# VectorE's order in the linear-attention loop: when the output is added to X, and when its statistics and moments are taken

## The chip, the cores and the metric

The kernel runs on one core of one Trainium2 chip, as one launch. The metric is the device time of that launch in microseconds. Before the change three runs took 624.18, 625.54 and 626.89 us; their median is 625.54 us.

## What is computed

A decoder block over x of shape 128 x 64 x 128 (batch, sequence, features), three sublayers, each added to x:

```
x = x + attention(layernorm(x))            # linear attention, 16 heads of 8, causal
x = x + correlation(layernorm(x), context) # lags picked from correlations, then mixed
x = x + moe(layernorm(x))                  # 8 experts, 2 for each row
```

The change lies in the first sublayer. For each head, with q, k passed through relu and exp and v plain:

```
S_t = sum over s <= t of k_s v_s^T ;  z_t = sum over s <= t of k_s
out_t = (q_t S_t) / (q_t z_t + eps) ;  x = x + out @ wo + bo
```

The correlation sublayer needs the mean and variance of the new x of each row, for its own layernorm.

## The kernel before

The 8192 rows are 64 tiles of 128 rows (two sequences in each), in 16 groups of 4 tiles. X, the running activations, stays in SBUF for all rows. Attention is a software pipeline over the groups, written by hand: each engine has a function `slot(n, i)`, called for n = -2 to 17 (slots 4 to 13 in a loop of two slots a turn, the others unrolled). In slot n an engine works on up to five groups at once: `a0` = n+2 (statistics and normalisation of the attention's input), `a1` = n+1 (transposes, projections, features, outer products), `b` = n (running sums over time and their product with q), `c` = n-1 (division, output product, add to X, statistics of the new X), `d` = n-2 (normalisation of the new X, keys, Gram matrices for the correlation sublayer). Each engine's instructions run in the order in which its `slot` writes them; engines meet through semaphores only.

What each engine does in a slot, as far as the prediction's steps touch it:

- TensorE (L1392): transposes of `xh` for a1 (L1353), running sums of tile 1 of b, projection 0, key sums, projection 1, transposes of `on` for c, running sums 2, keys of d, output product of c (which lets go `c_y`), projection 2, transposes of `xh` for d (the buffer `xh2`), running sums 3, projection 3, running sums 0 of the next group, Gram products of d (which wait for `c_x1`). All matrix products go through one helper and have line L1349.
- ScalarE (L681): evacuates the projections (L656 to L661), copies `xT` and `oT`, and normalises: `nb_a`, `xh` for a0, `nb_c`, `xh` for d (both through L675 and L678), which wait for GpSimd's roots `rs_a` and `rs_c`.
- GpSimd (L553): features `qk` (L540), outer products (L549), and between them the variances `ve_a`, `ve_c` (L525), each waiting for VectorE's moments, and the roots `rs_a`, `rs_c` (L531).
- VectorE (L965): for each tile of b a product `R` of the running sums with q (L899, `times_q`) and its sum over the head's elements `num` (L909, `sum_heads`). `R` is a single buffer: a product waits for the sum before it, and a sum for its own product. In between: reciprocals (L948) and quotients `on` (L954) of c, key dots `zq`, `den` of b (L915, L922), statistics and moments of a0 (L876, L884), the add of the output product to X (L962, `add_attention`, waits for `c_y`), and statistics and moments of the new X (L876, L884 with `st_c`, `mv_c`).

The running sums alternate between two PSUM buffers, so TensorE can be at most two tiles ahead of VectorE's products. Behind the 16 groups the correlation sublayer begins with a reduction over stored Gram matrices (`mean_early`), which needs the last group.

Of the kernel before, what the change touches and what calls it, by code (L numbers as in the profile page):

```python
# [55 lines left out]
def need(eng, sem, count):  # L56

    if not (isinstance(count, int) and count <= 0):
        eng.wait_ge(sem, count)
# [7 lines left out]
def build(nc, x, ctx_t, ctx_r, wqkv_p, b_all, wo, wq2, wk2, wv2t, wo2, bq2, bk2, bv2, scale, w_router, w_experts,  # L67
          tri, stri, ident, iota, dest, walk, place, late_in, out):
    with ExitStack() as ctx:
# [256 lines left out]
        def stage(n, i, shift):  # L326

            if i is None and not 0 <= n + shift < NG:
                return None
            return grp(n + shift, i)  # L330
# [503 lines left out]
        def _(dve):  # L834
            def fold_projection():

                dve.wait_ge(const_in, 64)
                dve.wait_ge(w_mean, 1)
                nc.vector.tensor_tensor(b_wide, b_wide, bank[1][:, 0:3 * E], ALU.subtract).then_inc(w_ch, 1)
                dve.wait_ge(w_ch, 1)  # L840
                nc.vector.scalar_tensor_tensor(wqkv[:], b_wide, 1.0 / E, wqkv[:], ALU.mult, ALU.add).then_inc(w_ch, 1)

            def fold_queries():

                nc.vector.tensor_reduce(q_shift[:, 0:1], wq2_s[:], AX.X, ALU.add).then_inc(kk_ch, 1)
                dve.wait_ge(kk_ch, 1)
                nc.vector.tensor_tensor(q_shift[:, 1:2], bq2_s[:], q_shift[:, 0:1], ALU.subtract).then_inc(kk_ch, 1)
                dve.wait_ge(kk_ch, 2)
                nc.vector.tensor_scalar(q_shift[:, 2:3], q_shift[:, 1:2], 1.0 / E, None, ALU.mult).then_inc(kk_ch, 1)
                dve.wait_ge(kk_ch, 3)  # L850
                nc.vector.tensor_scalar(wq2_s[:], wq2_s[:], q_shift[:, 2:3], None, ALU.add).then_inc(kk_ch, 1)

            def split_biases():

                n = 0

                def step(ins):
                    nonlocal n
                    n += 1
                    ins.then_inc(bias_ch, 1)  # L860
                    dve.wait_ge(bias_ch, n)
                step(nc.vector.tensor_copy(bias_p[0][:], bias_f))
                step(nc.vector.tensor_tensor(bias_r, bias_f, bias_p[0][:], ALU.subtract))
                step(nc.vector.tensor_copy(bias_p[1][:], bias_r))
                step(nc.vector.tensor_tensor(bias_a, bias_r, bias_p[1][:], ALU.subtract))
                step(nc.vector.tensor_copy(bias_p[2][:], bias_a))
                step(nc.vector.tensor_scalar(bias_b, bias_p[0][:], id_s[0:3, 0:1], None, ALU.mult))
                step(nc.vector.scalar_tensor_tensor(bias_r, bias_p[1][:], id_s[0:3, 1:2], bias_b, ALU.mult, ALU.add))
                dve.wait_ge(padded, 2)
                step(nc.vector.scalar_tensor_tensor(bias3[0:3, :], bias_p[2][:], id_s[0:3, 2:3], bias_r, ALU.mult, ALU.add))  # L870

            def stats(g, p, st, st_sem, mv, mv_sem, seen, per_group):
                need(dve, mv_sem, GT * g)
                settle(dve)
                for k in range(GT):
                    nc.vector.bn_stats(st[:, k, :], X[:, bass.ds(GT * g + k, 1), :].rearrange("p a b -> p (a b)")  # L876
                                       ).then_inc(st_sem, 1)

            def moments(g, p, st, st_sem, mv, mv_sem, seen, per_group):
                dve.wait_ge(st_sem, GT * g + GT)  # L880
                need(dve, seen, per_group * (g - 1))
                settle(dve)
                for k in range(GT):
                    nc.vector.bn_aggr(mv[p][:, k, :], st[:, k, :]).then_inc(mv_sem, 1)  # L884
# [9 lines left out]
            def times_q(g, p, r, k):  # L894
                t = GT * g + k
                need(dve, b_red, t)
                dve.wait_ge(b_run, t + 1)
                qq = qk[p][:, k, 0:E].rearrange("p (h d) -> p h d", h=H)
                nc.vector.tensor_tensor(  # L899
                    R[:, 0:D * E].rearrange("p (h e d) -> p h e d", h=H, e=D),  # L900
                    run[k % 2][:].rearrange("p (h e d) -> p h e d", h=H, e=D),
                    qq.unsqueeze(2).broadcast_to([P, H, D, D]), ALU.mult).then_inc(b_mul, 1)

            def sum_heads(g, p, r, k):
                t = GT * g + k
                dve.wait_ge(b_mul, t + 1)
                if k == 0:
                    need(dve, c_on, g - 1)
                nc.vector.tensor_reduce(num[p][:, k, :], R[:, 0:D * E].rearrange("p (x d) -> p x d", d=D), AX.X, ALU.add  # L909
                                        ).then_inc(b_red, 1)  # L910

            def key_dots(g, p, r):

                dve.wait_ge(b_keys, g + 1)
                nc.vector.tensor_tensor(  # L915
                    zq[:].rearrange("p (k c x) -> p c k x", k=GT, c=2), bank[4][:].rearrange("p (c k x) -> p c k x", c=2, k=GT),
                    qk[p][:, :, 0:E].rearrange("p k (c x) -> p c k x", c=2), ALU.mult).then_inc(b_dots, 1)

            def sum_dots(g, p, r):
                dve.wait_ge(b_dots, 2 * g + 1)  # L920
                need(dve, c_rden, g)
                nc.vector.tensor_reduce(den[:], zq[:].rearrange("p (x d) -> p x d", d=D), AX.X, ALU.add).then_inc(b_dots, 1)  # L922
# [21 lines left out]
            def inverses(g, p, r):  # L944
                dve.wait_ge(c_den, g + 1)
                need(dve, d_gd, g - 1)
                need(dve, c_x1, g)
                nc.vector.reciprocal(rden, den[:]).then_inc(c_rden, 1)  # L948

            def quotients(g, p, r):  # L950
                dve.wait_ge(c_rden, g + 1)
                need(dve, c_tr, g)
                dve.wait_ge(b_red, GT * g + GT)
                nc.vector.tensor_tensor(  # L954
                    on[:].rearrange("p t (h d) -> p (t h) d", h=H), num[p][:].rearrange("p t (h d) -> p (t h) d", h=H),
                    rden.unsqueeze(2).broadcast_to([P, GT * H, D]), ALU.mult).then_inc(c_on, 1)
# [8 lines left out]
            def slot(n, i):  # L965
                a0, a1, b, c = (stage(n, i, s) for s in (2, 1, 0, -1))
                if b:
                    times_q(*b, 0)
                    sum_heads(*b, 0)
                if c:  # L970
                    if i is None and c[0] == 0:
                        dve.wait_ge(kk_w, 1)
                    inverses(*c)
                if b:
                    times_q(*b, 1)
                if c:
                    quotients(*c)
                if b:
                    key_dots(*b)
                if a0:  # L980
                    g, p, r = a0
                    dve.wait_ge(x_in[p], 16 * r + 16)
                    stats(g, p, st_a, a_st, mv_a, a_mv, a_nb, GT)
                if b:
                    sum_heads(*b, 1)
                    sum_dots(*b)
                if a0:
                    moments(a0[0], a0[1], st_a, a_st, mv_a, a_mv, a_nb, GT)
                if i is None and n == FIRST:
                    fold_projection()  # L990
                    split_biases()
                if i is None and n == -1:
                    dve.wait_ge(w_in, N_W)
                    nc.vector.tensor_copy(bv2_wide[:], bv2_s[:, 0:1].broadcast_to([P, P])).then_inc(fold_wide, 1)
                    fold_queries()
                if i is None and n == NG:
                    split_fold()
                if b:
                    times_q(*b, 2)
                if c:  # L1000
                    add_attention(*c)
                if b:
                    sum_heads(*b, 2)
                if c:
                    dve.wait_ge(c_x1, c[0] + 1)
                    stats(c[0], c[1], st_c, c_st, mv_c, c_mv, c_nb, GT)
                if b:
                    times_q(*b, 3)
                if c:
                    moments(c[0], c[1], st_c, c_st, mv_c, c_mv, c_nb, GT)  # L1010
                if b:
                    sum_heads(*b, 3)

            slots(dve, slot)

            dve.wait_ge(w_in, N_W)
# [745 lines left out]
```

## Time and profile before

| | |
|---|---|
| median of the runs | 625.54 us |
| the profiled execution's own time | 626.32 us |
| its span, first to last instruction | 624.1 us |
| granted TensorE clock, mean | 0.979 |
| busy: TensorE, VectorE, ScalarE, GpSimd | 556.2, 504.1, 417.6, 407.6 us |

An engine's busy share says how much it does, not whether others wait for it; that is read from the idle times with their releasers, and from the chain of work that ended last. The attention stage fills the span's first 270 us.

### The profile page before, as it was taken

The page shows a single profiled execution, that of the slowest core. Times are in us where ns is not written, and L with a number is a line of the kernel's source. Part 1 is how long each engine was busy: PE and PEld are TensorE (multiplying, and loading weights), DVE is VectorE, ACT ScalarE, POOL GpSimd, SP SyncE. Part 2 cuts the span into 40 slices and gives each one's busy share as a digit, 9 for nine tenths or more (in the row PEclk, how much of TensorE's full clock was granted, in tenths as well). Part 3 has the DMA queues.
Part 4 walks back from the last instruction along what each step waited for, and adds up shares of the span by engine and source line. Part 5 has one row for each costly group of instructions (what it writes and reads, how often), then busy time and mean ns, then how long its engine had stood idle before and what let it go on. Part 6 is the DMA issues. An engine that isn't in the chain of part 4 may idle for free.

```text
span 624.1 us, 16569 instructions
## 1 busy us (share of the span) xinstructions
PE 556.2 (89%) x4286; PEld 407.8 (65%) x4287; DVE 504.1 (81%) x1506; ACT 417.6 (67%) x1188; POOL 407.6 (65%) x459
## 2 busy tenths in 40 slices
PE   4888999999999998878899786899999999999993
PEld 1333444444444444445888544799999999999993
DVE  4489999999999999874578988466887878877883
ACT  3556878888888775532888502445887888878882
POOL 2778888888888888112877501764566766757762
PEclk9979999999999999899999969999999999999998
DMA  5510111111161112362568480221111111111110
GB/s 153 187 50 2 35 35 36 35 34 34 34 101 34 34 37 65 67 137 57 159 196 206 78 137 5 59 51 38 35 50 51 47 44 47 52 40 51 52 45 22
DMA packets 49973, 40.99 MB, mean 66 GB/s; under 512 B 21971, under 2 KB 40278, under 8 KB 49926
## 3 DMA queue, kind: packets, MB, share of 16 engines
q1 hardware_dynamic: 44150, 29.68, 19.5%
q0 software_dynamic: 4960, 10.49, 6.4%
q8 instruction: 21, 0.34, 0.2%
q10 hardware_dynamic: 816, 0.26, 0.2%
q14 instruction: 26, 0.21, 0.1%
HBM read 27.54 MB, written 12.88 MB: 65 GB/s over the span
## 4 chain that ended last, share of the span: by engine, by line
PE 55%; ACT 16%; DVE 10%; issue 10%; POOL 4%; DMA 3%; ACTq 0%; SPq 0%; DVEq 0%; POOLq 0%
PE bank L1349 30%; PE run L1349 19%; ACT xh L678 4%; PE bank L1353 4%; ACT xs L780 2%; ACT ex L656 2%; DMA shared<-xs_d,row_u 2%; ACT nb_a L675 2%; PE run L1616 1%; ACT ex L661 1%; DVE mean_early L1057 1%; ACT xT L649 1%; PE run L1540 1%; DMA ct<-in_ctx_r 1%; ACT rl L657 1%
## 5 line engine op out<-in xcount | busy, mean ns | idle before, releaser
L616 POOL DMA_INDIRECT shared<-xs_d,row_u x91 | 87.8, 965 | 62.6 <-DVE row_u L1247 31.6
L549 POOL TENSOR_TENSOR shared<-v,qk 128x1024 f32<-128x1024 f32 x64 | 125.0, 1953 | 2.8
L623 POOL DMA_INDIRECT out_x<-shared x64 | 63.5, 992 | 48.2 <-DVE shared L1319 22.1
L899 DVE TENSOR_TENSOR R<-run,qk 128x1024 f32<-128x1024 f32 x64 | 77.5, 1210 | 12.5 <-PE run L1349 11.0
L1349 PE MATMUL bank<-wqkv,xT 128*64 128x128 f32 (+1 forms) x384 | 70.5, 353 | 15.5 <-ACT v L659 10.8
L1349 PEld LDWEIGHTS bank<-wqkv,xT 128*64 128x64 f32 (+1 forms) x384 | 33.4, 159 | 72.1 <-issue 37.4
L909 DVE TENSOR_REDUCE num<-R 128x128 f32<-128x1024 f32 x64 | 77.2, 1206 | 1.1
L1349 PE MATMUL run<-shared,tris_s 64*64 64x512 f32 x512 | 73.3, 644 | 0.0
L809 ACT ACTIVATE shared<-run,scale_s 128x128 f32<-128x128 f32 (+1 forms) x78 | 30.0, 385 | 41.5 <-PE run L1616 41.5
L540 POOL TENSOR_TENSOR qk<-ex,rl 128x256 f32<-128x256 f32 x64 | 46.5, 727 | 11.0 <-DVE mv_a L884 7.5
L656 ACT ACTIVATE ex<-bank 128x256 f32<-128x256 f32 x64 | 24.1, 376 | 28.9 <-PE bank L1349 28.9
L1349 PE MATMUL run<-w_s,hid 128*128 (+1 forms) x312 | 41.4, 275 | 0.0
L1349 PE MATMUL bank<-w_s,hid 128*128 (+1 forms) x308 | 41.1, 276 | 0.0
L813 ACT ACTIVATE ct<-w_s 128x512 f32 x64 | 39.8, 621 | 0.3 <-issue 0.3
L1340 DVE TENSOR_TENSOR hid<-run,shared 128x256 f32<-128x256 f32 x78 | 33.0, 423 | 8.3 <-ACT shared L819 7.9
L1349 PEld LDWEIGHTS run<-w_s,hid 128*128 128x128 f32 x312 | 38.0, 192 | 0.1
L1349 PEld LDWEIGHTS bank<-w_s,hid 128*128 128x128 f32 x308 | 37.6, 192 | 0.4 <-DVE hid L1340 0.2
L819 ACT ACTIVATE shared<-run 128x256 f32<-128x256 f32 x78 | 29.8, 382 | 10.9 <-PE run L1349 7.7
L819 ACT ACTIVATE shared<-bank 128x256 f32<-128x256 f32 x77 | 29.5, 383 | 10.9 <-PE bank L1349 8.6
L1340 DVE TENSOR_TENSOR hid<-bank,shared 128x256 f32<-128x256 f32 x77 | 32.5, 422 | 3.2 <-ACT shared L819 3.0
L1349 PE MATMUL run<-shared,ct 128*128 128x128 f32 x256 | 33.9, 275 | 0.0
L1349 PE MATMUL bank<-shared,ct 128*128 128x128 f32 x256 | 33.9, 275 | 0.0
(277 smaller groups left out, 1425.1 us busy)
## 6 DMA issues: line engine op xcount, KB each, us to landing
xs_d<-xs SPq DMA_DIRECT2D x16, 270.0 KB, 5.2
X<-in_x SPq DMA_DIRECT2D x16, 256.0 KB, 2.7
ct<-in_ctx_t SPq DMA_DIRECT2D x16, 256.0 KB, 3.0
ct<-in_ctx_r SPq DMA_DIRECT2D x16, 256.0 KB, 3.7
gram_d<-gd SPq DMA_DIRECT2D x14, 256.0 KB, 2.4
w_s<-in_w_experts SPq DMA_DIRECT2D x8, 384.0 KB, 3.9
circ<-prob_d SPq DMA_DIRECT2D x30, 64.0 KB, 2.8
shared<-xs_d,row_u POOLq DMA_INDIRECT x91, 2.6
```

The source lines that it names most:

```text
L540: nc.gpsimd.tensor_tensor(qk[p][:, k, :], ex[k % 2][:], rl[k % 2][:], ALU.add).then_inc(a_f, 1)
L549: nc.gpsimd.tensor_tensor(outer[k].rearrange("p (h e d) -> p h e d", h=H, e=D), vv.unsqueeze(3).broadcast_to([P, H, D, D]), kk.unsqueeze(2 ...
L616: nc.gpsimd.indirect_dma_start(xg[q], None, xs_d[:, :], bass.IndirectOffsetOnAxis(ap=rows, axis=0)).then_inc(xg_in[q], 16)
L623: nc.gpsimd.indirect_dma_start(out[:, :], bass.IndirectOffsetOnAxis(ap=xg[(NXI + j) % NX][:, DEST:DEST + 1].bitcast(U32), axis=0), yg[q], ...
L656: nc.scalar.activation(ex[k % 2][:], bank[1][:, HALF:HALF + 2 * E], ACT.Relu, scale=-1.0).then_inc(a_pev, 1)
L809: nc.scalar.activation(xgT[p][:, cols], bank[0][:, cols], ACT.Copy, scale=scale_s[:, 0:1]).then_inc(x_xT, 1)
L813: nc.scalar.activation(w_tile[n % 2][0], w_s[:, dyn(held[0] * W_E, 2 * HID)], ACT.Copy).then_inc(x_wa, 1)
L819: nc.scalar.activation(silu[p][h], bank[1 + 2 * p + h][:, HID:2 * HID], ACT.Silu).then_inc(x_silu, 2 // len(items_of(i, up[0])))
L899: nc.vector.tensor_tensor(R[:, 0:D * E].rearrange("p (h e d) -> p h e d", h=H, e=D), run[k % 2][:].rearrange("p (h e d) -> p h e d", h=H, ...
L909: nc.vector.tensor_reduce(num[p][:, k, :], R[:, 0:D * E].rearrange("p (x d) -> p x d", d=D), AX.X, ALU.add).then_inc(b_red, 1)
L1340: nc.vector.tensor_tensor(hid[p][h][:], bank[1 + 2 * p + h][:, 0:HID], silu[p][h], ALU.mult).then_inc(x_h, 2 // len(items_of(i, j)))
L1349: return nc.tensor.matmul(o, l, r, start=start, stop=stop, skip_group_check=True)
```

## The change

Only VectorE's `slot` changes. Nothing is added or removed; four things change places. The order of the second half of a slot was

times_q 2, add_attention, sum_heads 2, stats (new X), times_q 3, moments (new X), sum_heads 3

and becomes

times_q 2, sum_heads 2, add_attention, times_q 3, stats (new X), moments (new X), sum_heads 3.

```
                 if b:
                     times_q(*b, 2)
+                    sum_heads(*b, 2)
                 if c:
                     add_attention(*c)
                 if b:
-                    sum_heads(*b, 2)
+                    times_q(*b, 3)
                 if c:
                     dve.wait_ge(c_x1, c[0] + 1)
                     stats(c[0], c[1], st_c, c_st, mv_c, c_mv, c_nb, GT)
-                if b:
-                    times_q(*b, 3)
-                if c:
                     moments(c[0], c[1], st_c, c_st, mv_c, c_mv, c_nb, GT)
                 if b:
                     sum_heads(*b, 3)
```

Where b or c is missing (slot 0 and before, slots 16 and 17) the order stays as it was.

## Rows read from the trace of the kernel before

**Rows 1.** Busy time of each engine, 100 to 240 us, with clock and DMA share.
```profile
100.00:240.00 140.00, 130.24 (x932) 63.66 (x930) 133.80 (x268) 111.14 (x376) 121.81 (x114) 1.00 0.19 45
```

**Rows 2.** Shares of the chain of waits by line, 100 to 240 us.
```profile
by line: PE bank L1349 34.7%; ACT xh L678 12.2%; issue 11.6%; PE bank L1353 10.4%; ACT ex L656 4.5%; ACT ex L661 4.5%; PE run L1349 4.4%; ACT nb_a L675 3.8%; ACT xT L649 3.5%; ACT rl L657 2.5%; ACT gd L726 2.3%; ACT nb_c L675 1.6%; ACT den 
```

**Rows 3.** Time line of VectorE, slots 9 and 10: start, duration, line, operation.
```profile
164.55 1.19 DVE L899 TENSOR_TENSOR R<-run,qk 128x1024 f32<-128x1024 f32 x1
166.06 0.69 DVE L962 TENSOR_TENSOR X<-X,bank 128x512 f32 x1 [0.32 <-PE bank L1349]
166.67 1.21 DVE L909 TENSOR_REDUCE num<-R 128x128 f32<-128x1024 f32 x1
167.80 0.86 DVE L876 BATCH_NORM_STATS2 st_c<-X 128x6 f32 x4
168.57 1.21 DVE L899 TENSOR_TENSOR R<-run,qk 128x1024 f32<-128x1024 f32 x1
...
171.31 1.23 DVE L899 TENSOR_TENSOR R<-run,qk 128x1024 f32<-128x1024 f32 x1
172.65 1.22 DVE L909 TENSOR_REDUCE num<-R 128x128 f32<-128x1024 f32 x1
...
175.37 0.68 DVE L954 TENSOR_TENSOR on<-num,bank 128x512 f32<-128x512 f32 x1
...
179.06 0.37 DVE L884 BATCH_NORM_AGGREGATE mv_a<-st_a 128x2 f32<-128x6 f32 x4
...
183.38 1.21 DVE L899 TENSOR_TENSOR R<-run,qk 128x1024 f32<-128x1024 f32 x1
```

**Rows 4.** Idle time before the X add (L962): total us, times.
```profile
  PE bank L1349: 5.6, 13
```

**Rows 5.** Time line of slot 15: TensorE's transposes, VectorE's X add.
```profile
249.89 1.12 PE L1353 MATMUL bank<-id_s,on 128*128 128x128 f32 x4 [1.56 <-DVE on L954]
...
255.21 0.69 DVE L962 TENSOR_TENSOR X<-X,bank 128x512 f32<-128x512 f32 x1 [0.92 <-PE bank L1349]
```

**Rows 6.** Time line of TensorE, slots 9 and 10.
```profile
164.85 1.05 PE L1349 MATMUL bank<-wo_s,oT 128*128 128x128 f32 x8
...
167.27 1.09 PE L1349 MATMUL run<-shared,tris_s 64*64 64x512 f32 x8
...
170.77 0.69 PE L1349 MATMUL bank<-x2T,k2T 128*64 128x64 f32 x16
...
171.84 0.65 PE L1353 MATMUL bank<-id_s,xh 128*128 128x128 f32 x4 [0.39 <-ACT xh L678]
...
176.87 0.66 PE L1353 MATMUL bank<-id_s,on 128*128 128x128 f32 x4
...
182.16 1.09 PE L1349 MATMUL run<-shared,tris_s 64*64 64x512 f32 x8
```

**Rows 7.** Time line of VectorE, slot 16: statistics directly before moments.
```profile
265.58 0.87 DVE L876 BATCH_NORM_STATS2 st_c<-X 128x6 f32<-128x128 f32 x4 [0.19 <-DVE X L962]
266.64 0.38 DVE L884 BATCH_NORM_AGGREGATE mv_c<-st_c 128x2 f32<-128x6 f32 x4 [0.18 <-DVE st_c L876]
```

**Rows 8.** Time line of GpSimd: slot 0, then slots 9 and 10.
```profile
34.40 1.02 POOL L531 TENSOR_TENSOR rs_a<-ve_a,power 128x4 f32<-128x4 f32 x1
...
167.70 1.02 POOL L531 TENSOR_TENSOR rs_a<-ve_a,power 128x4 f32<-128x4 f32 x1
...
179.63 0.19 POOL L525 TENSOR_SCALAR ve_a<-mv_a 128x4 f32<-128x4 f32 x1 [1.73 <-DVE mv_a L884]
...
182.50 1.02 POOL L531 TENSOR_TENSOR rs_a<-ve_a,power 128x4 f32<-128x4 f32 x1
```

**Rows 9.** Time line of ScalarE: slot 0, then slots 9 and 10.
```profile
35.45 0.85 ACT L675 ACTIVATE nb_a<-mr_a,rs_a 128x1 f32<-128x1 f32 x4 [0.84 <-POOL rs_a L531]
...
169.32 0.85 ACT L675 ACTIVATE nb_a<-mr_a,rs_a 128x1 f32<-128x1 f32 x4
...
184.21 0.85 ACT L675 ACTIVATE nb_a<-mr_a,rs_a 128x1 f32<-128x1 f32 x4
```

More of the change, by code:

```diff
@@ L999, in slot @@
                     times_q(*b, 2)
+                    sum_heads(*b, 2)
                 if c:
@@ L1002, in slot @@
                 if b:
-                    sum_heads(*b, 2)
+                    times_q(*b, 3)
                 if c:
@@ L1006, in slot @@
                     stats(c[0], c[1], st_c, c_st, mv_c, c_mv, c_nb, GT)
-                if b:
-                    times_q(*b, 3)
-                if c:
                     moments(c[0], c[1], st_c, c_st, mv_c, c_mv, c_nb, GT)
```

## The prediction

> **What bounds the kernel now.** I read the busy shares of the attention loop first, then the chain of waits of the same stretch, then the time lines of the engines over two neighbouring slots, one odd (slot 9) and one even (slot 10), and last what the instructions at the changed place wait for. The change touches only slots in which both a group in its running-sum stage and a group in its output stage exist: slots 1 to 15. Between 100 and 240 us VectorE is busy 133.80 us of 140 and TensorE 130.24 [rows 1]; shares alone would name VectorE. The chain says otherwise: it consists of TensorE and ScalarE pieces (projection and its evacuations, `xh`, transposes), and no VectorE line is among its largest [rows 2]. The clock in that stretch is the full one, 1.00 of 2.4 GHz [rows 1]. One slot is the distance between the multiplications `R` of the third tile: 164.55 here, and the odd slot's X add at 166.06 carries the wait that the change wants to be rid of, 0.32 us for TensorE's output product [rows 3]. There are 13 such waits with 5.6 us in all over the stage [rows 4], and slot 15's alone is 0.92 [rows 5].
>
> **The changed order, priced on slot 9.** Before, VectorE starts: product 2 at 164.55, X add 166.06, sum 2 166.67, statistics 167.80, product 3 168.57, next slot's product 0 171.31 [rows 3]. The steps between independent neighbours are 1.13 us behind a product or a sum (166.67 to 167.80), 0.61 behind the X add, 0.77 behind four statistics: each is about 0.09 shorter than the instruction, because the next one starts before it has ended. Nothing is added or removed in count; three things change.
>
> (a) Sum 2 now stands right behind product 2, which it needs. Product 0 and sum 0 stand like that already: 171.31 to 172.65, 1.34 us instead of 1.13 [rows 3], so +0.21. X add then starts at 164.55 + 1.34 + 1.13 = 167.02. The output product's last record ends at 164.85 + 1.05 = 165.90 [rows 6] and before let the X add go at 166.06, 0.16 later; so the 0.32 wait is gone. VectorE would be ready for product 3 at 167.02 + 0.61 = 167.63, 0.94 earlier than before.
>
> (b) Product 3 can't use that. It reads the fourth tile's running sums, which TensorE makes from 167.27 to 168.36 [rows 6]; with the same 0.16 for the release it starts at 168.52, against 168.57 before. VectorE idles 0.89 us there. In slot 10 the sums end at 182.16 + 1.09 = 183.25 [rows 6], release 183.41, against 183.38 before [rows 3]: +0.03. This is the wait that takes the place of the one removed. TensorE's sums are in turn fed by nothing that the change brings forward: ahead of them stand the projection and the transposes of ScalarE's `xh`.
>
> (c) What was done while VectorE waited for those sums is now behind product 3: the statistics, and right behind them the moments, which need them. The trace has this pair adjacent, in slot 16: 265.58 to 266.64, 1.06 us, of which 0.18 is noted as idle for the statistics [rows 7]; between independent neighbours it is 0.77. So behind product 3 everything on VectorE starts 1.06 us later: in slot 9 by 1.06 - 0.05 = 1.01 us, in slot 10 by 1.06 + 0.03 = 1.09 us. Bounds for this lag: 0.77, if the gap of 0.29 is hidden, and 1.3, if the loop's register work adds as much again as the 0.21 of (a).
>
> The Trainium skill (VectorE: DVE Perf Modes, section The DRAIN you can't avoid) says that a semaphore between chained VectorE operations costs nothing extra, and its table advises to minimize the count of operations, not the semaphores. Here the trace does not agree: 1.34 against 1.13 and 1.06 against 0.77 for the dependent pairs. By that rule the lag would be 0.72 and 0.80, and the sum made below would be 1.4 + 0.76 = 2.1 us, a time of 627.7 instead of 629.7.
>
> **Who waits for VectorE once it is late by 1.0 to 1.1 us.** Queued behind product 3 and late by this lag are: moments of X, sum 3, and in the next slot product 0, sum 0, reciprocals, product 1, the quotients `on`, key dots, statistics and moments `mv_a`, up to product 2. There the lag ends, since 0.89 us of new idle time at product 3 absorbs it; it is made anew in each slot. Three consumers matter.
>
> TensorE's transposes of `on`: after slot 9 `on` ends at 175.37 + 0.68 = 176.05 and TensorE takes it at 176.87 [rows 3, 6]. The slack is 0.82 less a release; a lag of 1.01 costs about 0.2.
>
> GpSimd's variance waits for `mv_a` in every slot: 1.73 us of idle time ending at 179.63, 0.20 behind `mv_a`'s end at 179.43 [rows 3, 8]. So the lag passes whole into its outer product, features and `rs_a`. `rs_a` ends at 168.72 in slot 9 and 183.52 in slot 10 [rows 8], and ScalarE starts `nb_a` at 169.32 and 184.21 [rows 9]. A release from GpSimd to ScalarE shows as 0.03 (34.40 + 1.02 = 35.42, start 35.45) [rows 8, 9]. Slack: 0.57 in slot 9, 0.66 in slot 10. Behind `nb_a` the four `xh` follow, and TensorE waits 0.39 for them [rows 6], so whatever `nb_a` loses goes into the chain whole.
>
> TensorE's Gram product needs the X add, which now ends by 167.02 + 0.69 = 167.71, or 168.8 with the lag; it starts at 170.77 [rows 6], so two microseconds of TensorE's other work cover it. The moments `mv_c` end about 1 us later than before; GpSimd comes to them late by the same lag, as it is itself held by `mv_a`, so they cost nothing; if that failed, it would be at most the lag in one of GpSimd's pieces, some tenths a slot.
>
> **The sum.** A loop over two slots closes: product 3 of an even slot is late by 1.09 against TensorE, `nb_a` of the next slot by 1.09 - 0.57 = 0.52, that goes through `xh` into TensorE's queue, and the next even slot's running sums, hence its product 3, are 0.52 later. The path over `on` gives 0.2 a pair and runs beside it, hidden by the larger one; the odd slots' 1.01 - 0.66 = 0.35 is smaller than the shift already there. Slots 2 to 13 are six pairs: 6 x 0.52 = 3.1 us. (The first slots, still filling, may give less: bound 5 pairs, 2.6.) In slot 14 no new group is normalised, and slot 15's transposes of `on` wait for VectorE already, 1.56 us [rows 5]: the lag of slot 14, about 1.05, adds whole. In slot 15 the X add loses its wait of 0.92 [rows 5], the two gaps add 0.21 + 0.29 = 0.50, and product 3 may wait for its sums: between -0.4 and +0.5, taken as 0, because in slots 9 and 10 a freed wait is taken up by those sums. Sum: 3.1 + 1.05 = 4.2 us.
>
> The profiled execution took 626.3 (span 624.1 and 2.2 around it), the median of the runs is 625.5. So 630.5 for the profiled one and **629.7 us** for the median. With a lag of 0.8 the same sum gives 2.1, with 1.3 it gives 6 x 0.73 + 1.3 = 5.7: the forecast's own range is 627.6 to 631.2.
>
> **Rivals.**
> 1. Faster: VectorE sets the period, as its busy share suggests. Place: the X add; price: the 5.6 us of waits go, 619.9 us, if the gaps cost nothing; with 15 x 0.50 us of gaps it is +1.9 and no gain at all. It decides if product 3 is released about 0.9 us before the record of its sums allows and the gaps are small. For it: 133.80 busy of 140. Against: the chain has no VectorE, and product 3 already stands within 0.2 us of the end of its sums in both slots. Half of it would be 622.7.
> 2. No change: the lag is made, but ScalarE or GpSimd make it good before TensorE feels it, so that the loop over two slots doesn't close and only the end of the stage pays, 0 to 1.5 us: 625.5 to 627.0. For it: GpSimd has 1.73 us of idle time a slot. Against: that idle time lies ahead of `ve_a`, not behind it.
> 3. Much slower: TensorE, waiting longer in slot 15, runs more of its work at the lower clock. The transposes there took 1.12 us after an idle time of 1.56, against 0.66 for the same four in slot 10 [rows 5, 6]. Another microsecond of idle time could cost 1 to 2 us on top: 631 to 632.
>
> **Chances.** Forecast 0.55, rival 1 0.12, rival 2 0.23, rival 3 0.10. 0.5% is 3.1 us, what a measurement of this kernel can tell from no change. Of the forecast about three quarters lie above 628.7; with rival 3 that gives slower 0.50. Same is the rest of the forecast and rival 2, 0.38; faster is rival 1, 0.12. The range 624.5 to 632.0 holds the forecast, rival 2 and most of rival 3, and leaves out most of rival 1.
>
> **What would show it.** Right: the X add has no idle time in the loop; product 3 has 0.7 to 0.9 us of it per slot, released by TensorE's running sums; statistics to moments 1.0 to 1.1 us; `nb_a` waits for `rs_a` in odd slots; the slot is 14.8 us before (168.57 to 183.38) and near 15.1 after; GpSimd's idle time ahead of `ve_a` stays or grows. Wrong: if product 3 starts 0.9 us earlier against its running sums, step (b) is false; if statistics to moments is 0.9 or less, step (c) is too dear; if `nb_a` isn't late, the loop over two slots isn't there.

## The result, and the profile after

The changed kernel takes 629.14 us (median of 10 runs, 628.63 to 631.28) against 625.48 us before (10 runs). The ratio is 1.0059 with a 95% interval of 1.0037 to 1.0082: slower by 3.7 us. Forecast were 629.7 us and +4.2. The profiled execution has a span of 627.2 us, 3.1 more than before.

First the same busy row as in [rows 1], of the changed kernel, 100 to 240 us.

```profile
100.00:240.00 140.00, 126.47 (x919) 63.08 (x919) 134.34 (x268) 108.74 (x368) 120.09 (x112) 1.00 0.19 45
```

VectorE is as busy as before (134.34 us), TensorE is less so (126.47 for 130.24) at the same full clock: it waits more. Then the chain of the same stretch, of whose largest pieces in [rows 2] none was VectorE's or GpSimd's.

```profile
by line: issue 32.9%; DVE R L899 8.9%; ACT xh L678 7.7%; PE bank L1347 6.8%; POOL qk L540 5.2%; PE bank L1351 4.0%; DVE num L909 3.7%; POOL rs_a L531 3.5%; PE run L1347 3.4%; DVE st_a L876 3.0%; DVE st_c L876 2.5%; ACT ex L656 2.4%; POOL sh
```

Now VectorE's products, sums and statistics stand in it, and GpSimd's `qk` and `rs_a`. VectorE in the same two slots as in [rows 3]:

```profile
167.26 1.19 DVE L899 TENSOR_TENSOR R<-run,qk 128x1024 f32<-128x1024 f32 x1
...
168.49 1.22 DVE L909 TENSOR_REDUCE num<-R 128x128 f32<-128x1024 f32 x1
...
169.62 0.68 DVE L962 TENSOR_TENSOR X<-X,bank 128x512 f32 x1
...
170.44 1.22 DVE L899 TENSOR_TENSOR R<-run,qk 128x1024 f32<-128x1024 f32 x1
...
171.59 0.86 DVE L876 BATCH_NORM_STATS2 st_c<-X 128x6 f32 x4
...
172.63 0.38 DVE L884 BATCH_NORM_AGGREGATE mv_c<-st_c 128x2 f32<-128x6 f32 x4 [0.18 <-DVE st_c L876]
...
172.93 1.19 DVE L909 TENSOR_REDUCE num<-R 128x128 f32<-128x1024 f32 x1
...
174.24 1.22 DVE L899 TENSOR_TENSOR R<-run,qk 128x1024 f32<-128x1024 f32 x1
...
178.31 0.67 DVE L954 TENSOR_TENSOR on<-num,bank 128x512 f32<-128x512 f32 x1
...
182.27 1.19 DVE L899 TENSOR_TENSOR R<-run,qk 128x1024 f32<-128x1024 f32 x1
...
185.55 1.23 DVE L899 TENSOR_TENSOR R<-run,qk 128x1024 f32<-128x1024 f32 x1 [0.24 <-PE run L1347]
```

The X add has no idle time ahead of it (0.32 before). Statistics to moments are 1.04 us here and 1.10 in slot 10, as [rows 7] had 1.06. Product 3 stands at 170.44, where its running sums end at 169.29 + 1.09 = 170.38. Product 2 of slot 10 is late as well (182.27), and from product 3 to product 3 are 15.11 us, where [rows 3] had 14.81. What the other engines waited for in these slots:

```profile
169.29 1.09 PE L1347 MATMUL run<-shared,tris_s 64*64 64x512 f32 x8
...
171.46 0.85 ACT L675 ACTIVATE nb_a<-mr_a,rs_a 128x1 f32<-128x1 f32 x4 [0.22 <-POOL rs_a L531]
...
173.99 0.65 PE L1351 MATMUL bank<-id_s,xh 128*128 128x128 f32 x4 [0.52 <-ACT xh L678]
...
177.27 1.10 PE L1347 MATMUL bank<-qk,tris_s 128*128 128x256 f32 x4 [0.26 <-POOL qk L540]
...
182.55 0.19 POOL L525 TENSOR_SCALAR ve_a<-mv_a 128x4 f32<-128x4 f32 x1 [1.94 <-DVE mv_a L884]
...
184.39 1.09 PE L1347 MATMUL run<-shared,tris_s 64*64 64x512 f32 x8
```

ScalarE's `nb_a` now waits for `rs_a` in slot 9 (in [rows 9] it didn't), TensorE's transposes of `xh` wait 0.52 behind it (0.39 in [rows 6]), GpSimd waits longer for `mv_a` (1.94 after 1.73 in [rows 8]). One wait is new and I hadn't priced it: TensorE's key sums wait 0.26 for the features `qk` of the fourth tile, where before they waited for nothing in the loop. Another row will matter further on: the transposes of `on` start at 179.12, 0.14 behind the end of `on` (178.31 + 0.67). Where a wait for `on` is noted (moments of the input early, below), they start 0.15 behind it. The slack of this path, 0.82 before, is used up to its end. The pieces of the chain over two slots show the loop as a whole. The columns are start and length.

```profile
156.60 0.87 DVE st_c L876 x4
158.08 1.11 DVE num L909
159.31 1.23 DVE R L899
...
162.17 1.19 DVE R L899
164.69 0.66 DVE st_a L876 x3
...
169.73 0.73 POOL qk L540
170.45 0.98 POOL rs_a L531
172.61 0.83 ACT xh L678 x2
...
176.31 0.73 POOL qk L540
177.27 1.90 PE bank L1347 x10
179.17 0.60 PE bank L1351 x4
182.49 1.27 ACT xh L678 x3
...
184.46 1.06 PE run L1347 x8
...
186.69 0.88 DVE st_c L876 x4
```

From statistics to statistics are 186.69 - 156.60 = 30.09 us, two slots of the changed kernel; before they were 29.69 (X add of slot 4 to that of slot 12, four pairs: 91.80 to 210.56). The loop runs: statistics and sum 3 on VectorE, the next slot's products, the statistics of the new group, GpSimd's outer product and features, `rs_a`, ScalarE's `xh`, TensorE, GpSimd's features again, TensorE's key sums and transposes, `xh` of d, running sums 3, product 3.

The stage divided by VectorE's product 0 of slots 1, 4 and 14 and by the start of `mean_early`, us:

| kernel | slots 1 to 3 | slots 4 to 13 | slot 14 to `mean_early` | sum |
|---|---|---|---|---|
| before | 44.6 | 148.4 | 39.2 | 232.2 |
| changed | 46.3 | 150.4 | 39.8 | 236.5 |

4.3 us come up in this stage. The rest of the kernel is the same code and gave 1.2 of it back in this one execution. At the X add of slot 16 the changed kernel is at 268.89, before at 264.71: 4.2 us.

### The profile page after: what moved, and what is told of

It reads as the page before. It is cut to its first block, busy times and chain, and to the rows that moved or that the text cites. A ratio compares the mean times of both kernels' runs of the same rounds, so it can differ in the third digit from the quotient of the medians.

```text
span 627.2 us, 16569 instructions
## 1 busy us (share of the span) xinstructions
PE 554.3 (88%) x4286; PEld 408.5 (65%) x4287; DVE 507.0 (81%) x1506; ACT 417.7 (67%) x1188; POOL 407.3 (65%) x459
## 4 chain that ended last, share of the span: by engine, by line
PE 50%; DVE 17%; issue 13%; ACT 8%; POOL 6%; DMA 4%; DVEq 1%; POOLq 0%; ACTq 0%; SPq 0%
PE bank L1347 24%; PE run L1347 21%; DVE R L899 3%; ACT xh L678 2%; PE bank L1351 2%; ACT xs L780 2%; POOL qk L540 2%; PE run L1614 2%; DMA w_s<-gram_d 1%; DVE num L909 1%; POOL shared L549 1%; DVE mean_early L1055 1%; POOL rs_a L531 1%; DVE st_c L876 1%; PE run L1538 1%
## 5 line engine op out<-in xcount | busy, mean ns | idle before, releaser
L813 ACT ACTIVATE ct<-w_s 128x512 f32 x64 | 39.8, 621 | 0.3 <-issue 0.3
```

The costliest lines, as they stand in the source:

```text
L813: nc.scalar.activation(w_tile[n % 2][0], w_s[:, dyn(held[0] * W_E, 2 * HID)], ACT.Copy).then_inc(x_wa, 1)
```

## The experiments

All are compared with the kernel before on the same chip. "Two slots" is the mean distance of X adds of slots 4 to 12, from the profile. "Stage" is the sum of the three columns above and "end" the last of them. "Reduction" is where `mean_early` starts in the profiled execution; unlike "stage" it holds what happens before slot 1 as well. "Clock" is the granted TensorE clock between 240 and 262 us, slots 14 and 15 in the main, as a share of 2.4 GHz. Between 100 and 240 us it is 1.00 in all twelve.

| kernel | two slots | stage | end | reduction | clock | ratio, interval |
|---|---|---|---|---|---|---|
| before | 29.69 | 232.2 | 39.2 | 269.74 | 0.92 |  |
| changed | 30.10 | 236.5 | 39.8 | 274.11 | 0.92 | 1.0059, 1.0037 to 1.0082 |
| first half only | 29.61 | 233.8 | 40.2 | 271.40 | 0.92 | 1.0015, 0.9995 to 1.0035 |
| second half only | 30.10 | 235.2 | 40.0 | 272.59 | 0.92 | 1.0054, 1.0035 to 1.0073 |
| changed, moments last | 30.00 | 232.7 | 38.5 | 270.13 | 1.00 | 0.9997, 0.9981 to 1.0013 |
| changed, `mv_a` early | 30.08 | 237.3 | 40.2 | 273.95 | 0.92 | 1.0042, 1.0020 to 1.0065 |
| changed, variance later | 30.09 | 234.3 | 39.5 | 270.73 | 0.92 | 1.0026, 1.0002 to 1.0050 |
| changed, quotients early | 30.30 | 236.7 | 38.9 | 274.27 | 0.92 | 1.0058, 1.0035 to 1.0080 |
| changed, both of these | 29.94 | 231.1 | 37.3 | 267.09 | 1.00 | 0.9956, 0.9938 to 0.9975 |
| moments last, variance of X later | 29.82 | 233.8 | 40.6 | 271.33 | 0.84 | 1.0008, 0.9985 to 1.0032 |
| before, quotients early | 29.71 | 229.4 | 37.3 | 266.98 | 1.00 | 0.9963, 0.9938 to 0.9988 |
| first half, both edits | 29.86 | 230.3 | 36.8 | 266.38 | 1.00 | 0.9965, 0.9939 to 0.9990 |

Two things can be read off the table before any theory. The time follows the start of the reduction to within 1.6 us: with both of these edits it comes 2.65 us earlier and the kernel is 2.8 us faster. And the end of the stage goes with the clock. In the four kernels with 1.00 it takes 36.8 to 38.5 us, in the others 38.9 to 40.6. The rows for this stand behind the experiments.

**First half only.**

```diff
                 times_q 2
-                add_attention
                 sum_heads 2
+                add_attention
                 stats ; times_q 3 ; moments ; sum_heads 3
```

> Only the first half of the change: sum 2 stands before the X add, but statistics stay before product 3 and moments behind it. Theory A (the loop over two slots: what is late behind product 3 reaches GpSimd's rs_a and qk, ScalarE's xh and TensorE): the lag behind product 3 is some 0.1 us, under the slack of 0.5 to 0.67, so two slots of the loop take 29.7 us as before and the time is 625.5 us, ratio 0.998 to 1.002. Theory B (VectorE's own queue sets the new period by its length): the waits of 0.32 go, the gaps at sum 2 and at the statistics add about 0.4, so two slots take 29.7 to 29.8, ratio 1.000 to 1.003. Theory C (the later X add is what harms, by itself): two slots take 30.1 as in the changed kernel, ratio 1.006.

Measured: two slots 29.61, ratio 1.0015, an interval that holds 1. Moving the X add behind the sum does no harm in the loop; theory C falls. In the profile the stage is 1.6 us longer all the same: slots 1 to 3 take 1.0 more, the loop 0.4 less and the end 1.0 more. At the end the X add of slot 15 stands at 256.06, after 255.21 before, and the Gram products of that slot at 257.26 after 256.55. Their matrices go out and come back as the diagonal's load, which now lands last, while the X add of slot 16 is where it was (264.70 for 264.71):

```profile
271.40 7.10 DVE L1057 TENSOR_REDUCE mean_early<-w_s 112x64 f32<-112x4096 f32 x1 [1.59 <-DMA w_s<-gram_d]
```

**Second half only.**

```diff
                 times_q 2 ; add_attention ; sum_heads 2
+                times_q 3
                 stats
-                times_q 3
                 moments ; sum_heads 3
```

> Only the second half of the change: the X add stays before sum 2, statistics and moments both stand behind product 3. Theory A: the lag of about 1 us behind product 3 is the same as in the changed kernel, so two slots take 30.0 to 30.1 us, ratio 1.004 to 1.007. Theory B: VectorE's queue has the wait of the X add back or its own gap at product 3 instead of the one at sum 2, about as long: 30.0 to 30.1 too, ratio 1.004 to 1.007. Theory C: as before, 29.7, ratio 1.000.

Measured: 30.10 and 1.0054. The whole loss of the loop sits in the statistics behind product 3, as A and B said. Their times don't tell A and B apart, but the trace does. Product 3 waits in every slot of the loop, 0.27 to 0.36 us, for TensorE's running sums:

```profile
168.64 1.22 DVE L899 TENSOR_TENSOR R<-run,qk 128x1024 f32<-128x1024 f32 x1 [0.27 <-PE run L1349]
...
183.75 1.23 DVE L899 TENSOR_TENSOR R<-run,qk 128x1024 f32<-128x1024 f32 x1 [0.35 <-PE run L1349]
```

So the length of VectorE's queue is not what sets this period.

**Moments behind sum 3**, on the changed kernel (moments last).

```diff
                 times_q 3
                 stats
-                moments
                 sum_heads 3
+                moments
```

> The changed kernel with sum 3 between statistics and moments, so that the gap of 0.27 us ahead of the moments is filled; the moments of X themselves come 0.9 later, which should be covered. Theory A: the lag falls from about 1.0 to 0.75, two slots take 29.69 + 0.41 - 0.27 = 29.8, ratio 1.001 to 1.004. Theory B: the queue is 0.27 shorter in each slot, more than the whole excess, two slots 29.7, ratio 0.999 to 1.001. If the gap is of no account: 30.1, ratio 1.006.

Measured: the time is that of before (0.9997), and yet two slots take 30.00: neither theory's number. VectorE in an even slot, with what waited for it:

```profile
171.33 0.37 DVE L884 BATCH_NORM_AGGREGATE mv_c<-st_c 128x2 f32<-128x6 f32 x4
...
171.90 0.19 POOL L525 TENSOR_SCALAR ve_c<-mv_c 128x4 f32<-128x4 f32 x1 [0.49 <-DVE mv_c L884]
...
175.09 1.10 PE L1349 MATMUL bank<-qk,tris_s 128*128 128x256 f32 x4 [0.35 <-POOL qk L540]
...
183.36 1.23 DVE L899 TENSOR_TENSOR R<-run,qk 128x1024 f32<-128x1024 f32 x1 [0.70 <-PE run L1349]
```

Product 3 has 0.70 us of idle time, so VectorE's queue has room and its length is not the bound: theory B falls for this kernel. But the moments of X are now so late that GpSimd waits 0.49 for them ahead of an outer product, its features come late, and TensorE's key sums wait 0.35: a third route. I had priced the moments at nothing. The stage is 0.5 us longer than before: the loop lost 1.6, slots 1 to 3 gave back 0.4 and the end 0.7. At the end the granted clock stays at 1.00 in this kernel, for 0.92 before.

**Moments of the input early** (`mv_a` early), on the changed kernel.

```diff
                 sum_heads 1
+                moments (a0)
                 sum_dots
-                moments (a0)
```

> The changed kernel with the moments of the attention's input (mv_a) before the reduction of the key dots instead of behind it: mv_a is ready 0.6 us earlier, VectorE's queue keeps all its instructions. Theory A: mv_a's lag of 0.9 to 1.1 falls to 0.3 to 0.5, below both slacks, so the loop over two slots opens; what is left is the path over on, 0 to 0.25 for two slots: 29.7 to 29.9, and the lag at the end of the stage, 1.0 us. Ratio 1.001 to 1.004. Theory B: VectorE's queue is as long as in the changed kernel: 30.1, ratio 1.006.

Measured: two slots 30.08, no change, where A expected 29.7 to 29.9. `nb_a` no longer waits, but this does:

```profile
169.85 1.23 DVE L899 TENSOR_TENSOR R<-run,qk 128x1024 f32<-128x1024 f32 x1
...
177.72 0.67 DVE L954 TENSOR_TENSOR on<-num,bank 128x512 f32<-128x512 f32 x1
...
178.54 0.63 PE L1352 MATMUL bank<-id_s,on 128*128 128x128 f32 x4 [0.16 <-DVE on L954]
...
184.95 1.23 DVE L899 TENSOR_TENSOR R<-run,qk 128x1024 f32<-128x1024 f32 x1 [0.23 <-PE run L1348]
```

Product 3 to the end of `on` is 178.39 - 169.85 = 8.54 us, from there over the transposes (which wait 0.16 for `on`) to the next product 3 are 6.56: 15.10 for this slot, and 30.08 - 15.10 = 14.98 for the next. Theory B's number fits too, but product 3 has 0.23 us of idle time, so the queue is not full. The loop over `on` is as long as the one over `mv_a`; I had put it at 0.2 for two slots and hidden. Theory A as predicted, one route that holds the period, falls; A2, two routes of nearly the same length, is the next to test.

**Variance later**, on the changed kernel: GpSimd stops standing still for `mv_a`; VectorE's order is untouched.

```diff
                 features 0
-                variance (a0)
                 outer_product 0
+                variance (a0)
                 features 1
```

> The changed kernel; only GpSimd's order differs: outer product 0 before the variance of a0, so that GpSimd no longer stands still for mv_a, and rs_a and qk come up to 1.9 us earlier. VectorE's queue is untouched. Theory A as predicted (mv_a is the one route that closes the loop): two slots 29.7 to 29.8. Theory A2 (two routes of nearly the same length, mv_a and on): with this one cut, on alone holds the period, 30.05 to 30.1 for two slots, ratio 1.004 to 1.006; TensorE's transposes of on wait for VectorE in even slots. Theory B (length of VectorE's queue): 30.1 as well, but without TensorE waiting for on.

Measured: 30.09 for two slots, as A2 said. TensorE's transposes wait 0.18 us for `on` in slot 10, and product 3 has 0.23 of idle time there, so theory B isn't the reason. In the chain between 160 and 200 us, shown below, `on` has 5.1% and neither `qk` nor `rs_a` is among the largest. The ratio of 1.0026 lies below the 1.004 to 1.006 that I expected. Product 0 of slot 1 starts 1.2 us earlier than in the changed kernel (36.46 for 37.63) and slots 1 to 3 take 1.8 less (44.5 for 46.3): the edit also speeds up the filling of the pipeline, which has nothing to do with the loop.

```profile
by line: issue 20.5%; PE bank L1348 14.8%; PE run L1348 13.1%; PE bank L1352 9.6%; DVE R L900 9.3%; DVE st_c L877 6.6%; DVE num L910 5.9%; DVE on L955 5.1%; ACT xh L679 3.6%; DVE mv_c L885 2.8%; DVEq L877 1.7%; ACT nb_c L676 1.4%; ACT ex L6
```

**Quotients early**, on the changed kernel.

```diff
                 inverses
-                times_q 1
                 quotients
+                times_q 1
                 key_dots
```

> The changed kernel with VectorE's quotients before product 1 instead of behind it: on is ready about 1 us earlier, product 1 and all behind it up to mv_a 0 to 0.2 us later. Theory A2: the mv_a route is uncut, two slots 30.1 to 30.3, ratio 1.005 to 1.009. Theory C2 (on is the only route in fact): 29.7 to 29.8, ratio 1.001. Theory B: 30.1 to 30.4 (a gap more in the queue).

Measured: 30.30, ratio 1.0058. With only the `on` route cut nothing is won. The chain between 100 and 240 us has the other route instead, over `qk` and `rs_a`, and no `on` among the largest:

```profile
by line: issue 33.9%; ACT xh L678 7.7%; DVE R L899 7.0%; PE bank L1346 6.7%; POOL qk L540 5.2%; DVE num L909 3.7%; PE bank L1350 3.6%; POOL rs_a L531 3.5%; PE run L1346 3.0%; DVE st_a L876 3.0%; DVE st_c L876 2.5%; ACT ex L656 2.4%; POOL sh
```

**Both edits together**, variance later and quotients early, on the changed kernel.

> Both edits together: quotients before product 1 on VectorE, outer product 0 before the variance of a0 on GpSimd, on the changed kernel. Theory A2: both routes are gone, two slots fall to 29.7 to 29.9, held by TensorE and ScalarE or by VectorE's queue with its gaps (about 14.9 a slot); the end of the stage keeps its part: ratio 1.000 to 1.003. Theory B: 30.1 or more, ratio 1.006 or more.

Measured: two slots 29.94, just above the 29.7 to 29.9 of A2, and ratio 0.9956, faster than before and better than the 1.000 to 1.003 expected. Neither edit alone shortened the two slots, both together do, by 0.16: so there are two routes beside each other, A2. The chain of the loop is now VectorE's queue:

```profile
by line: issue 41.4%; DVE R L900 16.9%; DVE num L910 8.4%; DVE st_c L877 5.6%; DVE st_a L877 5.3%; PE bank L1347 3.5%; DVE bank L949 3.2%; DVE mv_c L885 2.4%; DVEq L877 2.4%; DVE mv_a L885 2.4%; PE run L1347 1.5%; DVE zq L916 1.2%; DVE den 
```

So about 14.97 us a slot is what VectorE needs with the gaps of this order, more than the 14.84 of before: 29.94 is its floor, and the excess over 29.69 that stays is theory B's, in this kernel only. Part of this floor comes from the edit itself. The quotients now stand right behind the reciprocals that they need, 0.70 us instead of the 0.46 to the product that stood there. In the changed kernel VectorE has idle time at product 3, so there the floor is not reached. The time is won outside the loop. Before slot 1 it is 1.6 us (product 0 of slot 1 at 35.95 for 37.58), in slots 1 to 3 it is 0.3 and at the end 1.9 (37.3 for 39.2), less the 1.2 lost in slots 4 to 13.

**Moments last and the variance of X later.**

```diff
                 features 2
-                variance (c)
                 outer_product 2
+                variance (c)
                 features 3
```

> The kernel with moments behind sum 3 (two slots 30.0 us there, GpSimd waiting 0.49 for mv_c), with GpSimd's outer product 2 before the variance of the new X. If the route over mv_c, features of tile 3 and the key sums holds its period, two slots fall to 29.7 to 29.8, 1.0 to 1.4 us for the stage, and the kernel is faster than the one before: 624.8, ratio 0.996 to 0.999. If on or mv_a hold it as well: 30.0, ratio 1.000.

Measured: two slots fall from 30.00 to 29.82, so the route over the moments of X was real. The ratio is 1.0008, where 0.996 to 0.999 was expected: the loop's gain of 0.9 us over ten slots was lost again at the end of the stage, which took 40.6 us for 38.5. From the X add of slot 14 to that of slot 15 alone are 16.84, for 14.79. The whole difference lies behind the transposes of `on`, from which to the X add are 6.62 us for 4.57, and there the granted clock is 0.50, as the rows below show. What holds the loop at 29.82 and not at 29.69 is open.

**Quotients early on the kernel before.**

> The kernel before with one edit: quotients before product 1. The run with both routes cut (ratio 0.9956) had a loop of 29.94 us for two slots, 0.25 above before, and yet was faster, since its slots 14 to 16 took 2.9 us less: TensorE waits for on there. If that is the reason, this kernel keeps the loop of before (29.7; VectorE's 0.32 of idle time a slot covers the new gap of about 0.24 ahead of the quotients) and takes 1.5 to 2.5 us off the end of the stage: ratio 0.995 to 0.998. If the gap is not covered: two slots 29.9 to 30.1, ratio 0.998 to 1.001.

Measured: two slots 29.71, ratio 0.9963. The gap ahead of the quotients is covered in the loop, as expected: the X add has no idle time left in even slots, and 0.32 still in odd ones. From the X add of slot 14 to that of slot 15 are 13.37 us for 15.23. This is the smallest edit that beats both kernels.

**First half of the change with both edits.**

> The kernel with sum 2 before the X add and statistics before product 3 (first half of the change, two slots 29.61 us), with both edits that cut the routes. By the theory of the two routes nothing is late behind product 3, and VectorE's queue of about 14.9 us a slot is the floor: two slots 29.7 to 29.9, the end of the stage as in the kernel with both routes cut: ratio 0.994 to 0.997. If the first half of the change cost something at the end of the stage again (the diagonal's load came 1.6 us late there): 0.997 to 1.000.

Measured: 29.86, ratio 0.9965, as expected; no better than the previous one.

**The clock in slot 15.** TensorE's transposes of `on` and the running sums behind them, in the kernel before, then in the kernel before with quotients early, then with moments last and the variance of X later. In the lines that begin with a stretch of time the third number from the end is the granted clock.

```profile
250.94 1.99 PE L1349 MATMUL run<-shared,tris_s 64*64 64x512 f32 x8
...
250.00:252.00 2.00, 2.00 (x12) 0.91 (x12) 2.00 (x3) 0.96 (x4) 0.04 (x1) 0.50 0.03 8
```
```profile
248.01 0.66 PE L1352 MATMUL bank<-id_s,on 128*128 128x128 f32 x4 [0.58 <-DVE on L954]
...
248.60 1.09 PE L1348 MATMUL run<-shared,tris_s 64*64 64x512 f32 x8
...
248.00:250.00 2.00, 1.84 (x13) 0.82 (x14) 2.00 (x3) 1.29 (x6) 1.15 (x1) 1.00 0.16 61
```
```profile
250.23 1.12 PE L1354 MATMUL bank<-id_s,on 128*128 128x128 f32 x4 [2.23 <-DVE on L955]
...
250.00:256.00 6.00, 5.77 (x18) 2.52 (x19) 4.94 (x6) 3.56 (x10) 0.00 (x0) 0.50 0.01 3
```

Before, TensorE waits 0.69 us for `qk` and, soon after, 1.56 for `on`. Then its granted clock is 0.50, which is 1.2 GHz. There the transposes take 1.12 us ([rows 5]) and the running sums 1.99, where at 1.00 they take 0.66 and 1.09. With the quotients early the wait for `on` is 0.58 and the clock stays at 1.00. From these transposes to the key products of d are 1.83 us instead of 2.96 (248.01 to 249.84, 249.89 to 252.85). So of the 1.86 us won between the two X adds about 1.1 come with the clock, and the shorter way to `on` gives about 1.0: the transposes start 8.92 us behind the X add of slot 14 instead of 9.91. Together that is 0.3 too much, since VectorE, and no longer TensorE, is then what product 2 waits for.

With moments last and the variance of X later the wait is 2.23 and the clock is 0.50 from 250 to 256 us. The wait for `on` alone doesn't decide it: in the changed kernel with quotients early it is 0.58 too, behind a wait of 1.74 for `qk`, and the clock falls. With both edits the same two waits stand there and it doesn't. What decides is open, and each of these readings is from one profiled execution.

## Why the prediction was right, point by point

- Bound before: right. The loop was TensorE's and ScalarE's, and the second half of the change broke that by making VectorE late against it. That this half alone gives 30.10 shows it.
- (a), the X add's wait goes: right, no idle time is left; the gap at sum 2 is 1.23 (167.26 to 168.49) where I took 1.34, 0.1 too dear.
- (b), the running sums take the place of the wait: right. Product 3 starts within 0.1 us of their end in both slots. The release is 0.06 us here, not the 0.16 taken from the X add.
- (c), 1.06 us behind product 3: right, 1.04 and 1.10.
- "There the lag ends, since 0.89 us of new idle time at product 3 absorbs it": wrong. Product 3 has no idle time in slot 1, 0.50 us in slot 2 and in the loop 0.24 in even slots. In odd slots none is noted, but it starts 0.82 behind the X add, where 0.59 to 0.61 is the step without a wait: about 0.2 there as well. The prediction kept product 2 where it was. Product 2 is late too: in slot 9 it starts 2.03 us ahead of the fourth tile's running sums, where before it was 2.72 (167.26 and 169.29 for 164.55 and 167.27). The forecast "0.7 to 0.9 us of idle time a slot" fell with it. It didn't touch the sum, since the loop was closed through the other engines.
- Route over `mv_a`, `rs_a`, `nb_a`, `xh`: seen in the chain; +0.41 for two slots against 0.52. The release of 0.16 makes 0.1 of the difference. Beside it, unforeseen, GpSimd's lateness also reaches the key sums through `qk`.
- Route over `on`, "0.2 a pair, hidden": mis-sized. Alone it holds the same 30.08; so the 0.41 doesn't depend on the `mv_a` route, and with that route cut the two slots stay as long. Only with both cut does the period fall. Part of the error was in reach: the slack was said to be 0.82 "less a release", and the release was then not taken off. With the 0.15 measured later, a lag of 1.01 costs 0.34, not 0.2.
- Moments of X at nothing: right for this change, but with little to spare: 0.9 us later they close a third route.
- End of the stage: slot 15's TensorE waits 1.57 for `on` as before (1.56 in [rows 5]), at 253.97 for 249.89, 4.1 us later; forecast were 3.1 + 1.05. Over the whole stage 4.3 for 4.2. That the whole agreed this well has luck in it: the loop gave 2.0 over slots 4 to 13 where five pairs at 0.52 are 2.6, slots 1 to 3 gave 1.7 including the first lag of 1.

The three rows of slots 14 and 15 on which this rests, of the changed kernel:

```profile
245.55 1.23 DVE L899 TENSOR_TENSOR R<-run,qk 128x1024 f32<-128x1024 f32 x1 [1.28 <-PE run L1347]
...
253.97 1.11 PE L1351 MATMUL bank<-id_s,on 128*128 128x128 f32 x4 [1.57 <-DVE on L954]
...
260.83 1.22 DVE L899 TENSOR_TENSOR R<-run,qk 128x1024 f32<-128x1024 f32 x1 [0.63 <-PE run L1347]
```

Product 3 of slot 14 had 1.28 us of idle time, that of slot 15 0.63: the wait that the X add lost in these slots (0.92 in slot 15) went to the running sums, as priced.

Rival 1 (VectorE's period, faster) fell by its own condition: product 3 starts 0.06 behind the record of its running sums and not 0.9 ahead. VectorE becomes the bound only where both routes are cut. Rival 3 (clock) didn't happen with this change: the transposes in slot 15 took 1.11 after 1.57 us of idle time, and the clock from 240 to 262 us is 0.92, both as before. The effect is real, though, and about as large as the rival had it: in five of the ten experiments the clock at the end is another than before, four times higher with a shorter end and once lower with a longer one. Rival 2 is refuted by the loop, which did close: 30.10 for 29.69.

## What to carry to other kernels

When an instruction is moved ahead of a wait, look at what now stands behind that wait: here the X add's wait of 0.32 us was gone, but the four statistics had moved behind the wait for the running sums, and what VectorE hands to GpSimd and TensorE came later in every slot. Slack has to be listed for every consumer, since two routes of the same length hide each other: cutting one doesn't shorten the loop, and only both together do. The chain of waits after each single cut names the one that is left. Read idle time per slot in the steady state: slot 2 of the new order showed 0.50 us at product 3, the loop half of that. And look at the whole kernel beside the loop. The kernels that ended up faster than before have no shorter loop; they won their time ahead of the loop and behind it, at the end together with the clock.

## What was unexpected of the hardware

Two VectorE instructions of which the second needs the first stand 0.1 to 0.3 us further apart than independent ones: 1.23 for 1.13 behind a product, 1.04 to 1.10 for 0.77 behind four statistics, 0.58 to 0.70 for 0.46 behind a reciprocal. In the order before, an independent instruction stood between statistics and moments and the gap was hidden. The differences between the kernels' loops, 0.1 to 0.6 us for two slots, are of that size. The same placement of quotients that gained nothing in the changed loop gained 1.9 us in one slot near the end of the stage (15.23 to 13.37), and about 1.1 of it goes with the granted clock, which stays at 1.00 there instead of falling to 0.50.
